# Gating the second expert layer on unscaled rows, and making its scaled rows later on two engines

## What is computed

```python
x = _layernorm(x + sa, g1, beta1)          # (x - mu) * rsqrt(var + EPS) * g + b
t = x.reshape(-1, D)
logits = t @ Wg + bg
idx = jnp.argmax(logits, axis=-1)
h = gelu(einsum('td,edh->teh', t, W1) + b1); y = einsum('teh,ehd->ted', h, W2) + b2
moe = einsum('ted,te->td', y, onehot(idx))
return _layernorm(x + moe, g2, beta2)
```

## Time and profile before

| | us |
|---|---|
| median of 3 runs | 1013.29 (1012.07 to 1017.85) |
| the profiled execution, its time | 1013.51 |
| its span in the profile | 1011.6 |
| VectorE: last tile sums end to first scaled row | 877.4 to 879.3 |
| VectorE: 16 operations of scaled rows | 879.3 to 890.0 |
| last low part of the transposed rows ends | 895.8 |
| first gate operation of VectorE | 899.6 |
| lists of rows ready | 908.9 |
| matmuls of the 15 blocks | 915.4 to 974.3 |

### The profile page before, as it was taken

The page is one execution under the profiler, slowest core; times in us unless marked ns, Lnnn a source line. Parts: engine busy times, 40 slices in busy tenths (PEclk is TensorE's granted clock), DMA queues, the critical chain, the costliest instruction groups (busy, mean ns, idle before and its releaser), DMA issues.

```text
span 1011.6 us, 13420 instructions
## 1 busy us (share of the span) xinstructions
PE 843.7 (83%) x4379; PEld 656.2 (65%) x4379; DVE 729.1 (72%) x1467; ACT 488.3 (48%) x887; POOL 351.1 (35%) x236
## 2 busy tenths in 40 slices
PE   2998999988729998699999798999999887547990
PEld 2776785367618884578888576777777665326850
DVE  8798988977984444983228588787787777895638
ACT  2257876445444552324032566566565655543530
POOL 1000000000223551033441466866867576504510
PEclk9999999999968997799999999999999999867985
DMA  6010000082433445342113300201100600653432
GB/s 172 22 34 1 1 2 1 1 292 71 165 125 110 155 137 203 130 122 66 52 42 114 84 1 21 53 11 21 32 10 12 187 1 1 213 193 103 148 144 96
DMA packets 55955, 84.73 MB, mean 84 GB/s; under 512 B 9024, under 2 KB 31808, under 8 KB 55504
## 3 DMA queue, kind: packets, MB, share of 16 engines
q1 hardware_dynamic: 49808, 63.94, 20.0%
q0 software_dynamic: 6080, 19.93, 6.1%
HBM read 57.11 MB, written 22.54 MB: 79 GB/s over the span
## 4 chain that ended last, share of the span: by engine, by line
PE 56%; DVE 31%; issue 4%; ACT 4%; DMA 2%; POOL 1%; DVEq 0%; SPq 0%; POOLq 0%; ACTq 0%
PE PS L335 37%; PE PS L2071 3%; DVE neg_max L1630 3%; PE PS L2086 3%; DVE APL L1016 3%; PE PS L2060 3%; PE PS L2085 3%; DVE late_columns L1207 2%; PE PS L1749 2%; PE PS L1910 2%; DVE stats L1024 1%; DVE early_columns L1207 1%; DVE XN L1704 1%; DVE stats L1483 1%; PE PS L1967 1%
## 5 line engine op out<-in xcount | busy, mean ns | idle before, releaser
L643 POOL TENSOR_SCALAR AP__204<-AP__204,rden 128x1024 f32<-128x1024 f32 x64 | 182.1, 2850 | 86.3 <-DVE rden L1635 85.3
L578 POOL TENSOR_TENSOR W1L<-W1R,W1H 128x1024 fp32r<-128x1024 f32 x8 | 19.7, 2498 | 250.8 <-DVE neg_max L1225 247.8
L675 ACT ACTIVATE APH<-PS 128x512 fp32r<-128x512 f32 x128 | 71.9, 598 | 69.7 <-PE PS L2071 45.3
L1630 DVE TENSOR_REDUCE neg_max<-PS 128x1 f32<-128x1024 f32 x64 | 78.2, 1223 | 34.3 <-PE PS L2060 33.5
L1016 DVE TENSOR_TENSOR APL<-PS,APH 128x512 fp32r<-128x512 f32 x128 | 83.0, 679 | 24.3 <-ACT APH L675 24.1
L335 PE MATMUL PS<-XTH,WH 128*128 128x512 f32 x224 | 80.6, 406 | 4.6 <-DVE XTL L1016 3.5
L2071 PE MATMUL PS<-ident,AP__204 128*128 128x128 f32 x512 | 71.4, 281 | 12.8 <-DVE APL L1016 12.0
L2071 PEld LDWEIGHTS PS<-ident,AP__204 128*128 128x128 f32 x512 | 59.6, 144 | 29.7 <-issue 17.6
L335 PE MATMUL PS<-XTL,WH 128*128 128x512 f32 x224 | 77.9, 394 | 0.0
L335 PE MATMUL PS<-XTH,WL 128*128 128x512 f32 x224 | 77.4, 392 | 0.0
L955 ACT ACTIVATE AP__204<-PS,neg_max 128x1024 f32<-128x1024 f32 x64 | 71.5, 1117 | 7.9 <-DVE neg_max L1630 7.2
(11 more groups left out here) (312 smaller groups left out, 2296.5 us busy)
## 6 DMA issues: line engine op xcount, KB each, us to landing
YT<-expert_rows SPq DMA_DIRECT2D x12, 512.0 KB, 6.6
counts<-CT SPq DMA_DIRECT2D x8, 512.0 KB, 4.9
W1R<-in_L_ffn_w SPq DMA_DIRECT2D x8, 512.0 KB, 5.2
W2R<-in_L_ffn_w SPq DMA_DIRECT2D x8, 512.0 KB, 5.6
normalised<-XN SPq DMA_DIRECT2D x2, 2048.0 KB, 8.6
CG<-counts SPq DMA_DIRECT2D x8, 512.0 KB, 3.5
RAW<-in_L_gnn_W SPq DMA_DIRECT2D x16, 256.0 KB, 2.7
W1R<-in_L_ffn_W SPq DMA_DIRECT2D x8, 512.0 KB, 7.4
```

The lines of the kernel that those rows point to most:

```text
L643: gp.tensor_scalar(AP_[:, i % 4, :], AP_[:, i % 4, :], rden[:, i % 4:i % 4 + 1], None, ALU.mult).then_inc(B["norm"], 1)
L675: act.activation(dst, src, Copy, **kw).then_inc(s, 1)
L1630: v.tensor_reduce(out=neg_max[:, i % 4:i % 4 + 1], in_=banks(2 * (i % 2)), axis=X_AXIS, op=ALU.max, negate=True).then_inc(B["mx"], 1)
```

## The change

The gate values of the second layer are computed from rows that are only normalised, `ZN = (x - mean) * rstd`. The scale g goes into the gate weights, and the product of the shift with the gate weights goes into the gate bias. The scaled and shifted rows, which the experts' matmuls and the last sum need, are made afterwards: tiles 0 to 3 by VectorE from `XN` after the low parts of the transposed rows, tiles 4 to 7 by GpSimd from `ZN`. GpSimd also makes one more low part of expert weights. `ZN` lies in the memory of `WL`, where the high parts of the second weights of experts 4 to 7 come later, so ScalarE waits for `n1` before experts 6 and 7.

```diff
-    POOL_LO = (3, 5)
+    POOL_LO = (3, 6)
+    norm_cols = const("norm_cols", [P, 2, KT], F32)
+    ZN = nc.alloc_sbuf_tensor_at("ZN", [P, NT, D], F32, offset=wl_offset)
# SyncE, among the early small loads
+            for m, n in enumerate(("L1_ffn_g1", "L1_ffn_beta1")):
+                sp.dma_start(norm_cols[:, m, :], a[n].rearrange("(k p) -> p k", p=P)).then_inc(norm_cols_in, 16)
# GpSimd, after the attention
         expert_lo(1)
+        wait(rows1_in, 32)
+        for t in range(4, NT):
+            wait(F["z"], t + 1)
+            gp.tensor_tensor(XN[:, t, :], ZN[:, t, :], rows1[:, 0, :], ALU.mult).then_inc(F["times_g"], 1)
+            wait(F["times_g"], t - 3)
+            gp.tensor_tensor(XN[:, t, :], XN[:, t, :], rows1[:, 1, :], ALU.add).then_inc(F["n1"], 1)
         expert_rows(1)
# ScalarE, in the first attention, and before the last two experts' second weights
-                copy(gws[:, :, :, 0:NEXP], gw[:, :, :, :], gw_hi)
+                copy(gws[:, 0, :, 0:NEXP], gw[:, 0, :, :], gw_hi)
+                act.wait_ge(norm_cols_in, 32)
+                for k in range(KT):
+                    copy(gws[:, 1, k, 0:NEXP], gw[:, 1, k, :], gw_hi, scale=norm_cols[:, 0, k:k + 1])
...
+            if which == 1:
+                act.wait_ge(F["n1"], NT)
             for e in range(6, NEXP):
                 w2_hi(e)
# VectorE, in the first attention
-        v.wait_ge(gw_hi, 1)
-        lo(gws[:, :, :, NEXP:2 * NEXP], gw[:, :, :, :], gws[:, :, :, 0:NEXP], gw_ready)
+        v.wait_ge(gw_hi, 1 + KT)
+        lo(gws[:, 0, :, NEXP:2 * NEXP], gw[:, 0, :, :], gws[:, 0, :, 0:NEXP], gw_ready)
+        for k in range(KT):
+            v.scalar_tensor_tensor(out=gws[:, 1, k, NEXP:2 * NEXP], in0=gw[:, 1, k, :], scalar=norm_cols[:, 0, k:k + 1],
+                                   in1=f(gws[:, 1, k, 0:NEXP]), op0=ALU.mult, op1=ALU.subtract).then_inc(gw_ready, 1)
# VectorE, moe
             transposed(turn, LTH, LTL)
-            weights_lo(which, 2 + which)
+            if which == 1:
+                rows_of_experts()
+            weights_lo(which, 2)
...
+            if which == 0:
+                v.tensor_tensor(gbias[:, 1, :], gbias[:, 1, :], PS[:, 2, P:P + NEXP], ALU.add).then_inc(M["gate_bias"], 1)
             weights_lo(which, 3 + which)
# VectorE, in place of scaled_rows(4, ...)
+        def rows_of_experts():
+            v.wait_ge(rows1_in, 32)
+            for t in range(5):
+                if t < 4:
+                    v.scalar_tensor_tensor(out=XN[:, t, :], in0=XN[:, t, :], scalar=mv[:, t, 0:1], in1=rows1[:, 0, :],
+                                           op0=ALU.subtract, op1=ALU.mult).then_inc(F["scaled"], 1)
+                if t:
+                    v.wait_ge(F["scaled"], t)
+                    v.scalar_tensor_tensor(out=XN[:, t - 1, :], in0=XN[:, t - 1, :], scalar=rstd[:, t - 1:t], in1=rows1[:, 1, :],
+                                           op0=ALU.mult, op1=ALU.add).then_inc(F["n1"], 1)
-        v.wait_ge(rows1_in, 32)
-        scaled_rows(4, rows1[:, 0, :], 0, lambda t: rows1[:, 1, :], F["n1"], XN)
+        norm_root(4)
+        for t in range(NT):
+            v.tensor_scalar(ZN[:, t, :], XN[:, t, :], mv[:, t, 0:1], rstd[:, t:t + 1], ALU.subtract, ALU.mult).then_inc(F["z"], 1)
         moe(3, 1, XN)
# TensorE, in the first expert layer after the gate values are transposed back
+            if which == 0:
+                for k in range(KT):
+                    pe.matmul(PS[:, 2, P:P + NEXP], norm_cols[:, 1, k:k + 1].to_broadcast([P, P]), gw[:, 1, k, :],
+                              start=k == 0, stop=k == KT - 1)
-        moe(3, 1, F["n1"], 0)
+        moe(3, 1, ZN, F["z"], 0)
```

More of the change, by code:

```diff
@@ L284, in build @@
     gw_hi, gw_ready = sem("gw_hi"), sem("gw_ready")
+    norm_cols_in = sem("norm_cols_in")
     def stage_semaphores(stage, names, **rings):
@@ L297, in build @@
     M = stage_semaphores("moe", "lg_ps gate_dve g_exp gates gt_ps gt g_ps acc routed route_ps w_hi w_lo b1_in "
-                         "xn_saved added x_ps x_hi x_lo h_ps h_b1 gelu t_ps t_hi t_lo y_ps y_sb w_lo_dve",
+                         "gate_bias xn_saved added x_ps x_hi x_lo h_ps h_b1 gelu t_ps t_hi t_lo y_ps y_sb w_lo_dve",
                          w_in=2, rows_in=3, rows_out=2, y_in=4)
@@ L309, in build @@
                          "cx_hi cx_lo y_ps yfree x_saved", q_twice=2, t_ps=2, t_hi=2, t_lo=2, pv_ps=2)
-    F = stage_semaphores("fin", "scaled n1 beta done out")
+    F = stage_semaphores("fin", "z times_g scaled n1 beta done out")
     wq = {0: a["L0_gnn_Wq"], 1: a["L1_ffn_Wq"]}
@@ L1288, in own @@
                 steps[0] += 1
+            if which == 1:
+                v.wait_ge(M["gate_bias"], 1)
             lg = PS[:, 7, 0:NT * 2 * NEXP].rearrange("p (t j e) -> p t j e", t=NT, j=2)
@@ L1718, in _ @@
         v.wait_ge(rows1_in, 48)
-        scaled_rows(5, g2_row[:, :], NT, lambda t: X[:, t, :], F["done"], X)
+        scaled_rows(5, g2_row[:, :], 4, lambda t: X[:, t, :], F["done"], X)
     @block.tensor
@@ L1858, in _, with moe @@
         values(NT // 2 - 1, 1)
-        def moe(turn, which, ready, before):
-            transposes(turn, XN, ready, before)
+        def moe(turn, which, src, ready, before):
+            transposes(turn, src, ready, before)
             if which == 0:
-                pe.wait_ge(gw_ready, 1)
+                pe.wait_ge(gw_ready, 1 + KT)
             for half in range(2):
@@ L1968, in moe @@
                           start=True, stop=True).then_inc(M["g_ps"], 1)
-        moe(1, 0, LN["xn"], NT)
+        moe(1, 0, XN, LN["xn"], NT)
         for t in range(NT):
```

## The result

| | us |
|---|---|
| before, median of 20 runs | 1011.79 (1010.28 to 1017.85) |
| changed, median of 20 runs | 1015.88 (1011.96 to 1018.54) |
| ratio | 1.0027, 95% interval 1.0016 to 1.0039 |
| profiled execution of the changed kernel, span | 1015.9 |

The executions of each kernel spread over about 7 us, and the quotient of the two medians would be 1.0040; the ratio with its interval is the number to use. By it the change costs 2.7 us, 1.6 to 3.9. In a second comparison, further down, the ratio was 1.0022.

What follows compares the result with a forecast made beforehand. VectorE's unbroken sequence from shift row to lists was taken to bound the changed stretch. Its stages summed to +0.85, plus +0.4 in the first attention: +1.25 us, forecast 1014.5, range 1009.0 to 1018.5.

Steps and rivals of the forecast that it cites:

- rival one: VectorE and GpSimd do not get in each other's way in the changed stretch: -4.4 us, 1008.9; chance 0.2.
- Rivals two and three: Two: late save delays gathers, up to 1018.9, chance 0.15. Three: four tiles hidden, gate values used when ready, 1008.0, chance 0.05.
- last variance to first normalised row: Root stage on VectorE: shift-row wait goes, -0.6; second step waits for GpSimd's sixth low part, +0.25.
- normalised in place of scaled rows: VectorE's eight operations at 3.65 us in place of 16 at 10.69, -7.0; held beside GpSimd, +2.5.
- low parts of transposed rows: VectorE's eight low parts come without a gap, 4.87 us in place of 5.75: -0.9.
- four tiles by VectorE, with turns: Eight scaled-row operations on VectorE after the low parts, +5.3; waiting and taking turns with GpSimd, +2.9.
- weights and idle time: Before the gate operation, VectorE makes two low parts of weights in place of three, -1.1; idle time goes, -0.5.
- gate weights in the first attention: Four more VectorE operations of 8 elements, on the path: +0.4 us (to +0.7).
- The root: Before the first row, only its second step, reading SBUF twice, waits for GpSimd's sixth low part: +0.25 (0 to 0.3).
- The upper end: Normalised rows: each of the last two finds GpSimd inside an operation of 1.24 us, +2.5; the lower end costs nothing.
- The saving of the wait for the shift row: Before the root, VectorE's wait of 0.61 us for the shift row goes: -0.6.

Runs made afterwards that it cites:

- second comparison: The unedited changed kernel timed again beside the other kernels, against the kernel before: ratio 1.0022 (1.0003 to 1.0040), 2.2 us.
- the kernel with five low parts: Changed kernel with GpSimd making five low parts of weights in place of six, VectorE three: stretch 22.84 us in one profile.
- the second of before: The kernel before profiled again without an edit: span 1011.0 us, stretch 21.84 us.
- The small parts alone: Kernel before plus the change's loads, gate-weight copies and low parts, shift matmuls and bias addition, results unused: ratio 1.0006 (0.9990 to 1.0023).
- the best version: Changed kernel with two low parts later, five on GpSimd, two tiles on GpSimd, gate-weight operations and first bias moved; against before: 0.9979 and 0.9936.

## Why the prediction came out as it did

**The mechanism was right, and shown.** The change was forecast to cost about as much as it saves, because the two engines exclude each other; it did. Rows 5 to 7 were read as exclusion, each waiting for the operation in which the other is. Without GpSimd's products VectorE loses no time, with GpSimd writing only it loses none on operations with two sources, and rival one, which would have given 1008.9, is out: its terms came back as 4.1 us when GpSimd's work was taken away. Rivals two and three did not occur either: the first gather waited for the lists, and the gate values waited for VectorE.

**The terms**, forecast and measured in the first profile:

| | forecast | measured |
|---|---|---|
| last variance to first normalised row | -0.35 | +0.59 |
| normalised in place of scaled rows | -4.5 | -6.0 |
| low parts of transposed rows | -0.9 | -1.0 |
| four tiles by VectorE, with turns | +8.2 | +8.4 |
| weights and idle time | -1.6 | -1.6 |
| sum | +0.85 | +0.44 |
| gate weights in the first attention | +0.4 | +0.5 |

The last two rows of the stretch come from 10.68 less 3.86, with 2.28 for the two low parts. Two terms were mis-sized, the root by +0.9 and the normalised rows by -1.5. That the sum of the stretch came out within 0.4 us is in part luck.

The root: I let only its second step wait for GpSimd's sixth low part, because it reads SBUF twice. The first step, with one source in SBUF, was held already, 1.2 to 1.35 us in every kernel with six low parts and 0.17 in those with five. The same rule that I used for the normalised rows would have given it.

The normalised rows: I had two of GpSimd's operations come between the last three, +2.5. It was one, +0.95, in the changed kernel's three profiles, and two, +1.9, in the kernel with five low parts. GpSimd's first product started half a microsecond after its tile was ready, at 885.86 with the fifth row ended at about 885.4, one row later than I had it. The upper end was a real case, but not the likelier one. One of the eight took 1.49 us beside 0.54 for the others. The Trainium skill's statement (VectorE: DVE Perf Modes, Mode 2×_2P) that such an operation uses both read ports agrees with that.

The saving of the wait for the shift row, -0.6, was in one profile of before only; the others have 0.1. Against the second of before (21.84) the stretch grew by 0.6 to 1.0, and not by 0.44.

**What stays open.** Over these profiles the stretch and the gate weights make +0.8 to +1.5 us. The two comparisons give 2.7 (1.6 to 3.9) and 2.2 (0.3 to 4.0), and no stage holds the rest: at about the same granted clock, what is left of the span without the two was no longer in the changed kernel (978.1 and 977.6) than before (979.1 and 978.9). The small parts alone, 1.0006, do not exclude it either.

The granted clock may hold it. Over the 75 executions of the kernel before that were timed beside the experiments, the time grows by 0.5 us when the mean granted clock falls by 0.001 (correlation -0.69). Their mean is 0.929; the changed kernel had 0.926 in the twenty executions of the first comparison and 0.927 in the twelve of the second. An estimate from these, for the second comparison: 0.9 us of the 1.4 by which the means differ. Whether the change lowers the clock, or the executions were drawn so, is not shown; no run was made for it.

The last attention, which the change doesn't touch, takes 280.9 to 281.2 us in six of the fourteen profiles and 281.8 to 282.5 in eight: in one of four of kernels in the old order, in five of eight with the changed one, and in both of the best version. The three longest, 282.3 to 282.5, are the three with a mean granted clock of 0.920 or 0.921, and the only ones in which the clock is below 0.9 in the slice in which the attention begins (the 23rd of 40). The line of the first profile of the changed kernel, then of its second:

```profile
PEclk9999999989968997799999899999999989867985
PEclk9999999999869997799999999999999989867985
```

## What to carry to other kernels

Before work is given to GpSimd because it is idle, look at what VectorE does at that time: beside operations with two sources in SBUF, or quick one-source operations in SBUF, a GpSimd operation that reads cost VectorE about 1 us of its 1.24 (0.95 for one, 3.17 for three), so 5.3 us taken over were worth 1.0 to 1.3. Put GpSimd's part under a stretch of VectorE that reads PSUM, and make it no longer than that stretch. When a result comes earlier than its user is free, as the gate values did by seven microseconds, the gain is in the user's order of work, and 2.3 us of the stretch were had by moving two operations.

## What the runs showed of the hardware

A VectorE operation of 8 elements with one source and its output in SBUF took 1.17 to 1.35 us beside a GpSimd subtraction and 0.17 without. GpSimd fills, 0.52 us each, did not slow VectorE's operations with two sources in SBUF (0.75 each, as alone), and slowed the eight with one source by 0.6 us in all. That agrees with the Trainium skill (SBUF — State Buffer, Who interferes with whom), by which a VectorE instruction with two SBUF inputs contends with a GpSimd instruction that reads SBUF and not with one that only writes it, and one in a two-port mode, which needs one source and the output in SBUF, contends with GpSimd in either case.

Where both engines stood in line they alternated in each profile: VectorE's operations started 1.7 us apart in place of 0.66, GpSimd's 1.6 to 1.8 apart in place of 1.24 to 1.35, and none went twice while the other waited.
